# A scan kernel: halving the slots of a product on GpSimd before VectorE sums them

## The chip, the cores and the metric

One core of a Trainium2 chip runs the whole program. The time is device microseconds (us) of one execution. The engines named below are TensorE (PE, with its weight loads PEld), VectorE (DVE), ScalarE (ACT), GpSimd (POOL) and the queue of DMA transfers on SyncE (SP).

## What is computed

The reference is a chain of an image network, an attention, a mixture of experts, a memory layer trained at test time and a second mixture of experts. The change lies in the memory layer, a scan over 96 tokens for a batch of 32. Cut to its core:

```python
def loss_fn(params, kk, vv):
    pred = _mlp(params, kk)
    return jnp.mean((pred - vv) ** 2)

def step(carry, xs):
    cp, cm = carry
    k_t, v_t, q_t, a_t, th_t, e_t = xs
    g = jax.vmap(jax.grad(loss_fn))(cp, k_t, v_t)
    s = lambda c: c[:, :, None]
    nm = jax.tree_util.tree_map(lambda m, gg: m * s(e_t) - s(th_t) * gg, cm, g)
    np_ = jax.tree_util.tree_map(lambda p, m: p * (1.0 - s(a_t)) + m, cp, nm)
    out_t = jax.vmap(_mlp, in_axes=(0, 0))(np_, q_t)
    ...
```

`_mlp` is two matrix products with a silu between them. The kernel never forms the weights of the later steps: each gradient is an outer product, so it keeps the vectors (the hidden gradients dz, the hidden values h and the output gradients dy) and adds up their weighted contributions.

## The kernel before, in words

The scan is `memory_scan`, L1378 to L1926. The 96 steps are cut into 6 chunks of 16 (chunk 0 to 5); within a chunk the place of a step is its slot, 0 to 15. Contributions of earlier chunks come from TensorE. Contributions of the chunk's own earlier slots come from elementwise work over a history tile with 16 slots per value: in slot i, n = max(i, 1) slots count. The batch is worked in two halves, g = 0 and g = 1, which leapfrog: while one half waits for TensorE or ScalarE, VectorE works on the other.

VectorE takes its instructions in the order in which they are written. One step (`one_step` of the vector block) issues: silu of half 1 (L1748 to L1751); `output` and `output_end` of half 0 (L1733 to L1739, L1760 to L1805); `hidden_before` of half 0 for the next step (L1718, L1719); `output` of half 1; `gradient_scores` of half 0 (the second L1733 to L1739); `hidden_before` of half 1; `output_end` of half 1; then the gradients, and the hidden values and the silu of half 0 of the next step.

`hidden_before` is the reader that matters here. It waits for a semaphore of GpSimd and sums a product over its slots:

```python
dve.wait_ge(zprod_ready, 2 * (t - c - 1) + g + 1)
n = max(t - c * NC - 1, 1)
s.link(V.reduce_sum(zsum[:, g, :], z_prod[:, g, :, :].rearrange("p a (b s) -> p (a b) s", s=NC)[:, :, 0:n], AX.X))
s.mark(V.tensor_tensor(quads(z_before[:, g, :]), quads(zsum[:, g, :]), base_at(g, t), ALU.add))
```

GpSimd writes that product. Its step (`one_step` of the gpsimd block, L1506 to L1536) issues, also in order: from chunk 1 on two small weights `wm` (L1511); the two `y_w` (L1519, each after VectorE's L1803 has read the previous one); for each half two products `prod` with the new hidden value (L1525), their sum (L1528), and the slope of the silu (L1529 to L1532); and last the two products `z_prod` (L1536), 32 values by n slots, for the next step. L1525 to L1528 already use a semaphore `halves_ready` for the order of a product and a sum on GpSimd itself.

TensorE's order in a step is forward scores of half 0, forward past 0, forward scores 1, backward scores 0 (which waits for L1805 of half 0), forward past 1, backward past 0, backward scores 1, backward past 1. VectorE waits for forward past at L1792 and for backward scores at the second L1733.

Of the kernel before, what the change touches and what calls it, by code (L numbers as in the profile page):

```python
# [7 lines left out]
ALU = mybir.AluOpType  # L8
# [11 lines left out]
def bc(ap, *shape):  # L20

    return ap.broadcast_to(list(shape))
# [1061 lines left out]
NC = 16  # L1084
# [293 lines left out]
def memory_scan(nc, M, H_room, hist_y, ident, cols_in, rows_in, own_in):  # L1378
# [12 lines left out]
    GW = QB * NC  # L1391
    APART = 4
    with ExitStack() as ctx:
# [10 lines left out]
        hist_h, hist_dz = sb("hist_h", [128, 2, 2, NB, NC]), sb("hist_dz", [128, 2, 2, NB, NC])  # L1404
# [5 lines left out]
        prod, z_prod = (room[:, n * 1024:(n + 1) * 1024].rearrange("p (g a x) -> p g a x", g=2, a=2) for n in range(2))  # L1410
# [4 lines left out]
        g_row = sb("g_row", [128, 2, NB * NC])  # L1415
# [22 lines left out]
        upto = lambda x, g, c, n: x[:, c % 2, :, :, 0:n].rearrange("p a (c b) s -> p a c b s", c=2)[:, :, :, QB * g:QB * (g + 1), :]  # L1438
        part = lambda x, n: x.rearrange("p (b s) -> p b s", s=NC)[:, :, 0:n]
        four = lambda x, n: x.rearrange("p a (c b s) -> p a c b s", c=2, s=NC)[:, :, :, :, 0:n]  # L1440
        over = lambda x, n: bc(x.rearrange("p (c b s) -> p c b s", c=2, s=NC)[:, :, :, 0:n].unsqueeze(1), 128, 2, 2, QB, n)
# [6 lines left out]
        summed, zprod_ready, dz_ready, pool_step, wm_ready = sem("summed"), sem("zprod_ready"), sem("dz_ready"), sem("pool_step"), sem("wm_ready")  # L1448
        halves_ready = sem("halves_ready")
# [11 lines left out]
        with nc.Block() as block:  # L1461
            @block.sync
            def _(sp):
                sp.dma_start(cols[:, :, :], cols_in).then_inc(ones_in, 16)
                sp.dma_start(rows_[:, :, :], rows_in).then_inc(ones_in, 16)
                sp.dma_start(own[:, :], own_in).then_inc(ones_in, 16)
                for c in range(NCH):
                    def rows(k, t, turn):
                        if turn is not None:
                            sp.wait_ge(yw_ready, 2 * turn)  # L1470
                            sp.wait_ge(z_ready, 2 * turn)
                        for b2 in range(2):
                            sp.dma_start(w_row[b2 * DM:(b2 + 1) * DM, k, :],
                                         M["w_rows"][bass.ds(t, 1), c, b2 * HB:(b2 + 1) * HB, :].rearrange("t b s -> t (b s)").broadcast_to([DM, HB * NC])).then_inc(w_in[k], 16)
                        sp.dma_start(g_row[:, k, :], M["g_rows"][bass.ds(t, 1), c, :, :].rearrange("t b s -> t (b s)").broadcast_to([128, NB * NC])).then_inc(g_rows_in[k], 16)

                    if c == 0:
                        for k in range(2):
                            rows(k, k, None)
                        with sp.Fori(1, NC // 2) as i:  # L1480
                            for k in range(2):
                                rows(k, 2 * i + k, 2 * i + k - 1)
                    else:
                        with sp.Fori(0, NC // 2) as i:
                            for k in range(2):
                                rows(k, c * NC + 2 * i + k, c * NC + 2 * i + k - 1)
                for n in range(2):
                    sp.wait_ge(dumped[n], 16 * NCH)

            @block.gpsimd  # L1490
            def _(pool):
                P = nc.gpsimd
                for t in (hist_h, hist_dz):
                    P.memset(t[:, :, :, :, :], 0.0).then_inc(zeroed, 1)
                P.memset(hist_y[:, :, :, :], 0.0).then_inc(zeroed, 1)
                P.memset(dy_now[:, :, :, :], 0.0).then_inc(zeroed, 1)
                P.memset(y_prod[:, :, :], 0.0).then_inc(zeroed, 1)
                P.memset(room[:, 0:1024], 0.0).then_inc(zeroed, 1)
                pool.wait_ge(zeroed, 6)
                pool.wait_ge(ones_in, 48)  # L1500
                for c in range(NCH):
                    pool.wait_ge(g_rows_in[0], (c * NC // 2) * 16 + 16)
                    if c >= 2:
                        pool.wait_ge(zeroed, 6 + c - 1)

                    def one_step(i, k, last):  # L1506
                        t, n = c * NC + i, max(i, 1)
                        if c >= 1:
                            pool.wait_ge(dz_ready, 2 * t - 2)
                            for g in range(2):  # L1510
                                ins = P.tensor_tensor(wm[:, k, g, 0:c, :].rearrange("p c (q b) -> p c q b", q=2),  # L1511
                                                      bc(M["w_bs"][:, 0:c, :, t:t + 1].rearrange("p c (q h) t -> p c q (h t)", q=2)[:, :, :, g:g + 1], 128, c, 2, QB),
                                                      bc(own[:, :].unsqueeze(1).unsqueeze(1), 128, c, 2, QB), ALU.mult)
                                ins.then_inc(wm_ready, 1)
                        pool.wait_ge(w_in[k], (t // 2) * 32 + 32)
                        for g in range(2):

                            pool.wait_ge(yprod_ready, 2 * t + g + 1)
                            P.tensor_tensor(part(y_w[:, g, :], n), part(w_row[:, k, g * GW:(g + 1) * GW], n), hist_y[:, c, g * QB:(g + 1) * QB, 0:n], ALU.mult).then_inc(yw_ready, 1)  # L1519
                        for g in range(2):  # L1520
                            pool.wait_ge(h_ready, 2 * t + g + 1)
                            pool.wait_ge(h_stored, 2 * t if i else 2 * t + g + 1)
                            now = h_now[:, g, 0, :].rearrange("p (a c b) -> p a c b", a=2, c=2).unsqueeze(4)
                            for a in range(2):
                                ins = P.tensor_tensor(four(prod[:, g, :, :], n)[:, a], upto(hist_h, g, c, n)[:, a], bc(now[:, a], 128, 2, QB, n), ALU.mult)  # L1525
                            ins.then_inc(halves_ready, 1)
                            pool.wait_ge(halves_ready, 2 * t + g + 1)
                            P.tensor_tensor(four(prod[:, g, :, :], n)[:, 0], four(prod[:, g, :, :], n)[:, 0], four(prod[:, g, :, :], n)[:, 1], ALU.add).then_inc(prod_ready, 1)  # L1528
                            P.tensor_tensor(hg[:, g, :], h_now[:, g, 0, :], sg[:, g, :], ALU.mult)  # L1529
                            P.tensor_tensor(hs[:, g, :], h_now[:, g, 0, :], sg[:, g, :], ALU.add).then_inc(pool_step, 1)  # L1530
                            pool.wait_ge(pool_step, 2 * t + g + 1)
                            P.tensor_tensor(slope[:, g, :], hs[:, g, :], hg[:, g, :], ALU.subtract).then_inc(slope_ready, 1)  # L1532
                        if not last:
                            pool.wait_ge(g_rows_in[1 - k], ((t + 1) // 2) * 16 + 16)
                            for g in range(2):
                                P.tensor_tensor(four(z_prod[:, g, :, :], n), upto(hist_dz, g, c, n), over(g_row[:, 1 - k, 2 * GW * g:2 * GW * (g + 1)], n), ALU.mult).then_inc(zprod_ready, 1)  # L1536

                    for i in range(NC):
                        one_step(i, i % 2, i == NC - 1)
                    if 1 <= c < NCH - 1:  # L1540
                        pool.wait_ge(dumped[(c - 1) % 2], 32 * ((c - 1) // 2 + 1))
                        pool.wait_ge(turned, 5 * c)
                        P.memset(hist_dz[:, (c + 1) % 2, :, :, :], 0.0).then_inc(zeroed, 1)
# [151 lines left out]
            def _(dve):  # L1695
# [3 lines left out]
                s = Steps(dve, step)  # L1699
# [11 lines left out]
                for c in range(NCH):  # L1711
                    base_at = lambda g, t: M["z_base"][:, :, :, bass.ds(t, 1)].rearrange("p a (c b) s -> p a c (b s)", c=2)[:, :, :, QB * g:QB * (g + 1)]

                    def hidden_before(s, g, t):

                        dve.wait_ge(zprod_ready, 2 * (t - c - 1) + g + 1)
                        n = max(t - c * NC - 1, 1)
                        s.link(V.reduce_sum(zsum[:, g, :], z_prod[:, g, :, :].rearrange("p a (b s) -> p (a b) s", s=NC)[:, :, 0:n], AX.X))  # L1718
                        s.mark(V.tensor_tensor(quads(z_before[:, g, :]), quads(zsum[:, g, :]), base_at(g, t), ALU.add))  # L1719

# [129 lines left out]
                    if c >= 1:  # L1850
# [22 lines left out]
                        for j, (src, parts, left) in work:  # L1873
                            dve.wait_ge(mid_ready, 4 * (c - 1) + j + 1)
                            dve.wait_ge(rest_ready, 4 * (c - 1) + j + 1)
                            ins = V.tensor_tensor(parts(2), left, parts(1), ALU.subtract)
# [11 lines left out]
                    s = Steps(dve, step, start)  # L1888
# [313 lines left out]
```

## Time and profile before

| what | us |
|---|---|
| median of 3 runs (4443.79 to 4450.76) | 4450.04 |
| the profiled execution | 4450.9 |
| its span, first to last instruction | 4448.7 |
| scan, first to last step on the trace, about | 2403 to 3969 |
| busy in the whole span: PE, PEld, DVE, ACT, POOL | 3744.6, 3132.7, 2504.3, 549.9, 740.6 |

The shares over the whole span mix stages: the image network takes the first 40% and the scan about 35%. The scan is looked at by itself, chunk by chunk, and inside a chunk by the timeline of two engines side by side.

### The profile page before, as it was taken

The page shows a single profiled execution, that of the slowest core. Times are in us where ns is not written, and L with a number is a line of the kernel's source. Part 1 is how long each engine was busy: PE and PEld are TensorE (multiplying, and loading weights), DVE is VectorE, ACT ScalarE, POOL GpSimd, SP SyncE. Part 2 cuts the span into 40 slices and gives each one's busy share as a digit, 9 for nine tenths or more (in the row PEclk, how much of TensorE's full clock was granted, in tenths as well). Part 3 has the DMA queues.
Part 4 walks back from the last instruction along what each step waited for, and adds up shares of the span by engine and source line. Part 5 has one row for each costly group of instructions (what it writes and reads, how often), then busy time and mean ns, then how long its engine had stood idle before and what let it go on. Part 6 is the DMA issues. An engine that isn't in the chain of part 4 may idle for free. (4 is left out here: it accounts for less than half of the span.)

```text
span 4448.7 us, 109537 instructions
## 1 busy us (share of the span) xinstructions
PE 3744.6 (84%) x44268; PEld 3132.7 (70%) x44268; DVE 2504.3 (56%) x8138; ACT 549.9 (12%) x1173; POOL 740.6 (17%) x1900
## 2 busy tenths in 40 slices
PE   6999999999999999697656566687998878859587
PEld 5898988769989887454424455687997778857444
DVE  4454545145455452223756888888787887852413
ACT  0101011310010112211211110101001000001011
POOL 1000000000000000000002434334343332332021
PEclk9999999999999999777855555555555555556589
DMA  1010000000000000100003110111000000021111
GB/s 37 16 17 2 16 2 16 2 6 16 2 16 16 2 1 2 25 0 4 0 10 91 32 35 29 31 29 31 26 25 32 22 29 24 22 75 46 21 39 27
DMA packets 189736, 96.97 MB, mean 22 GB/s; under 512 B 139463, under 2 KB 172535, under 8 KB 188632
## 3 DMA queue, kind: packets, MB, share of 16 engines
q1 hardware_dynamic: 183574, 84.19, 8.1%
q10 hardware_dynamic: 4626, 7.39, 0.4%
q8 instruction: 147, 2.41, 0.2%
q0 software_dynamic: 1280, 2.10, 0.2%
q14 instruction: 109, 0.89, 0.1%
HBM read 76.11 MB, written 15.96 MB: 21 GB/s over the span
## 5 line engine op out<-in xcount | busy, mean ns | idle before, releaser
L349 PEld LDWEIGHTS im_acc<-im_cwt,im_chan 128*128 128x128 f32 x2048 | 268.7, 191 | 123.0 <-issue 117.3
L468 ACT ACTIVATE im_a<-im_acc 128x512 f32<-128x512 f32 x256 | 152.9, 597 | 1376.7 <-PE im_acc L349 1376.7
L204 POOL DMA_DIRECT2D image_rows<-im_ho x16 | 9.6, 603 | 1761.2 <-DVEq L459 1761.2
L445 DVE COPY im_chan<-im_ring 128x512 f32<-128x512 f32 x192 | 132.8, 692 | 286.8 <-PE im_ring L296 286.8
L346 PE MATMUL im_acc<-im_u,im_e 97*128 97x512 f32 x512 | 265.3, 599 | 7.6 <-DVE im_u L439 7.6
L349 PE MATMUL im_acc<-im_cwt,im_chan 128*128 x2048 | 270.1, 274 | 0.0
L258 PE MATMUL im_ring<-im_d,im_a 128*128 128x128 f32 (+1 forms) x2048 | 242.5, 281 | 19.1 <-issue 12.9
L258 PEld LDWEIGHTS im_ring<-im_d,im_a 128*128 128x128 f32 x2048 | 239.5, 198 | 22.1 <-issue 18.5
L1641 PE MATMUL sc_ps<-H,sc_cols 128*128 128x128 f32 x768 | 231.2, 457 | 11.9 <-POOL H L1528 11.5
L439 DVE COPY im_u<-im_ring 80x512 f32<-80x512 f32 x256 | 171.6, 685 | 118.8 <-PE im_ring L290 118.8
L406 DVE COPY im_half_t<-im_ring 128x480 f32<-128x480 f32 x192 | 168.5, 903 | 116.5 <-PE im_ring L258 116.5
L1662 PE MATMUL sc_ps<-sc_y_prod,sc_rows 128*128 128x128 f32 x768 | 230.6, 456 | 0.0
L290 PE MATMUL im_ring<-im_e,im_half_t 80*80 80x128 f32 x2048 | 229.0, 273 | 0.0
L290 PEld LDWEIGHTS im_ring<-im_e,im_half_t 80*80 80x80 f32 x2048 | 224.6, 150 | 0.4
L1525 POOL TENSOR_TENSOR H<-sc_hist_h,sc_h_now 128x16 f32<-128x16 f32 (+14 forms) x384 | 147.7, 404 | 462.8 <-DVE sc_h_now L1748 365.9
L1648 PE MATMUL sc_ps<-sc_coef_y,sc_dy_t 128*128 128x16 bf16 x2880 | 105.4, 176 | 116.8 <-DVE sc_coef_y L1739 116.3
L1648 PEld LDWEIGHTS sc_ps<-sc_coef_y,sc_dy_t 128*128 128x128 bf16 x2880 | 99.5, 106 | 147.1 <-DVE sc_coef_y L1739 142.6
L1575 ACT ACTIVATE sc_sg<-sc_z 128x32 f32<-128x32 f32 x192 | 43.9, 229 | 1271.1 <-DVE sc_z L1726 1236.8
L296 PE MATMUL im_ring<-ident,im_a 128*128 128x128 f32 x1280 | 192.8, 280 | 1.4 <-ACT im_a L468 1.4
L1641 PEld LDWEIGHTS sc_ps<-H,sc_cols 128*128 128x128 f32 x768 | 178.2, 322 | 14.9 <-POOL H L1528 14.4
L277 PE MATMUL im_ring<-im_spec,im_wbd 128*128 128x128 f32 x1600 | 180.7, 275 | 0.0
L277 PEld LDWEIGHTS im_ring<-im_spec,im_wbd 128*128 128x128 f32 x1600 | 179.3, 192 | 1.1 <-issue 0.2
(394 smaller groups left out, 7460.3 us busy)
## 6 DMA issues: line engine op xcount, KB each, us to landing
sc_g_row<-mem_g_rows_dram SPq DMA_DIRECT2D x96, 256.0 KB, 3.5
im_wbd<-in_c_mix_dram SPq DMA_DIRECT2D x32, 400.0 KB, 6.1
sc_w_row<-mem_w_rows_dram SPq DMA_DIRECT2D x192, 64.0 KB, 2.5
sw_g_all<-sw_gates SPq DMA_DIRECT2D x8, 768.0 KB
mem_hist_h_dram<-sc_hist_h ACTq DMA_DIRECT2D x6, 512.0 KB, 3.0
mem_hist_dz_dram<-sc_hist_dz ACTq DMA_DIRECT2D x6, 512.0 KB, 3.7
mo_hist_dz<-mem_hist_dz_dram SPq DMA_DIRECT2D x8, 384.0 KB, 6.4
mo_hist_h<-mem_hist_h_dram SPq DMA_DIRECT2D x8, 384.0 KB, 6.5
```

The lines of the kernel that those rows point to most:

```text
L258: mm = MM(ps[:, i * 80:i * 80 + n], a[:, g, c, :], d1[:, 0:n], start=True, stop=True)
L277: mm = MM(ps[:, i * 32:i * 32 + 128], wbd[:, m, :], spec[:, m:m + 4, :].rearrange("p m b -> p (m b)"), start=True, stop=True)
L290: mm = MM(ps[0:80, i * 128:(i + 1) * 128], half_t[0:80, g % 2, (q + i) * 80:(q + i + 1) * 80], e1[:, :], start=True, stop=True)
L296: mm = T(ps[:, m * 128:(m + 1) * 128], a[:, g, :, :].rearrange("p c (w x) -> p (c w) x", x=32)[:, :, p * 4 + m], ident[:, :])
L346: MM(acc[:, p % 2, :], e2[0:97, :], u[:, p, :, :].rearrange("p o w -> p (o w)"), start=True, stop=True, skip_group_check=True)
L349: mm = MM(acc[:, p % 2, m:512:4], chan[:, p % 2, m * 128:(m + 1) * 128], cwt[:, bass.ds(l, 1), :].rearrange("p a c -> p (a c)"), start=Fal ...
L406: V.tensor_copy(half_t[:, g % 2, :].rearrange("p (n c) -> p c n", c=C)[:, q:q + w, :], src).then_inc(drained, 1)
L439: V.tensor_copy(u[0:80, :, q:q + 4, :], src).then_inc(drained, 1)
L468: nc.scalar.activation(a[:, g, :, :].rearrange("p c (w x) -> p (c w) x", x=32)[:, :, p * 4:p * 4 + 4], acc[:, p % 2, :].rearrange("p (c m) ...
L1641: mm = MM(hh(g), cols[:, b2, :], prod[:, g, 0, b2 * GW:(b2 + 1) * GW], start=b2 == 0, stop=b2 == 1)
L1648: mm = MM(past_y(g), dy_t[:, cc, w, g, :], top(coef_y[:, g, m, cc, :]), start=n == 0, stop=n == 6 * c - 1)
L1662: mm = MM(yy(g)[:, b2 * GW:(b2 + 1) * GW], rows_[:, b2, :], y_prod[:, g, :], start=True, stop=True)
```

## The change

After the two products `z_prod` of a slot with n of 4 or more, GpSimd adds the upper n // 2 slots onto the lower n // 2, for each half in two instructions (a = 0, 1). VectorE's reduction then reads only n - n // 2 slots. The products count on `halves_ready`, which orders GpSimd's adds behind them, and the second add of a half counts on `zprod_ready`, for which VectorE waits. `halves(t)` is the number of counts before step t. For n below 4 nothing changes.

```diff
+                    halves = lambda t: 2 * t + 2 * (NC - 5) * (t // NC) + 2 * max(t % NC - 4, 0)
+
                     def one_step(i, k, last):
...
-                            pool.wait_ge(halves_ready, 2 * t + g + 1)
+                            pool.wait_ge(halves_ready, halves(t) + g + 1)
...
                             for g in range(2):
-                                P.tensor_tensor(four(z_prod[:, g, :, :], n), upto(hist_dz, g, c, n), over(g_row[:, 1 - k, 2 * GW * g:2 * GW * (g + 1)], n), ALU.mult).then_inc(zprod_ready, 1)
+                                P.tensor_tensor(four(z_prod[:, g, :, :], n), upto(hist_dz, g, c, n), over(g_row[:, 1 - k, 2 * GW * g:2 * GW * (g + 1)], n), ALU.mult).then_inc(halves_ready if n >= 4 else zprod_ready, 1)
+                            for g in range(2 if n >= 4 else 0):
+                                slots = lambda a, lo, hi: z_prod[:, g, a, :].rearrange("p (b s) -> p b s", s=NC)[:, :, lo:hi]
+                                pool.wait_ge(halves_ready, halves(t) + 2 + g + 1)
+                                for a in range(2):
+                                    ins = P.tensor_tensor(slots(a, 0, n // 2), slots(a, 0, n // 2), slots(a, n - n // 2, n), ALU.add)
+                                ins.then_inc(zprod_ready, 1)
...
                         n = max(t - c * NC - 1, 1)
+                        n = n - n // 2 if n >= 4 else n
                         s.link(V.reduce_sum(zsum[:, g, :], z_prod[:, g, :, :].rearrange("p a (b s) -> p (a b) s", s=NC)[:, :, 0:n], AX.X))
```

GpSimd's order at slot 14 of chunk 2, before (`H` is the room that `prod` and `z_prod` share):

```order
L1529 TENSOR_TENSOR sc_hg<-sc_h_now,sc_sg 128x32
L1530 TENSOR_TENSOR sc_hs<-sc_h_now,sc_sg 128x32
L1532 TENSOR_TENSOR sc_slope<-sc_hs,sc_hg 128x32
L1536 TENSOR_TENSOR H<-sc_hist_dz,sc_g_row 128x32x14 x2
L1511 TENSOR_TENSOR sc_wm<-mem_w_bs,sc_own 128x32 x2
L1519 TENSOR_TENSOR sc_y_w<-sc_w_row,hist_y 128x8x15 x2
```

The same place with the change:

```order
L1531 TENSOR_TENSOR sc_hg<-sc_h_now,sc_sg 128x32
L1532 TENSOR_TENSOR sc_hs<-sc_h_now,sc_sg 128x32
L1534 TENSOR_TENSOR sc_slope<-sc_hs,sc_hg 128x32
L1538 TENSOR_TENSOR H<-sc_hist_dz,sc_g_row 128x32x14 x2
L1543 TENSOR_TENSOR H<-H 128x16x7 x4
L1513 TENSOR_TENSOR sc_wm<-mem_w_bs,sc_own 128x32 x2
L1521 TENSOR_TENSOR sc_y_w<-sc_w_row,hist_y 128x8x15 x2
```

Four adds of 16 by 7 elements stand between the products and the next step's `wm` and `y_w`.

In chunk 0, which has no `wm`, the same slot with the change reads:

```order
L1531 TENSOR_TENSOR sc_hg<-sc_h_now,sc_sg 128x32
L1532 TENSOR_TENSOR sc_hs<-sc_h_now,sc_sg 128x32
L1534 TENSOR_TENSOR sc_slope<-sc_hs,sc_hg 128x32
L1538 TENSOR_TENSOR H<-sc_hist_dz,sc_g_row 128x32x14 x2
L1543 TENSOR_TENSOR H<-H 128x16x7 x4
L1521 TENSOR_TENSOR sc_y_w<-sc_w_row,hist_y 128x8x15 x2
```

Here the adds stand right ahead of `y_w`. On the other engines the order is as before; on VectorE L1718 reads fewer slots.

## Rows read from the trace of the kernel before

**Rows 1.** Busy time by stretch, here chunks 0, 2 and 3 (columns in the first line).

```profile
core 0: us, PE busy (x) PEld busy (x) DVE busy (x) ACT busy (x) POOL busy (x), PEclk, DMA share, GB/s
2403.00:2582.00 179.00, 95.56 (x944) 76.07 (x944) 151.06 (x697) 26.14 (x73) 84.56 (x239) 0.50 0.13 34
2859.00:3106.00 247.00, 204.79 (x4882) 188.82 (x4883) 206.68 (x1026) 19.24 (x73) 98.21 (x287) 0.52 0.09 26
3134.00:3390.00 256.00, 242.29 (x6472) 231.10 (x6468) 202.55 (x971) 22.21 (x76) 95.24 (x269) 0.51 0.09 28
```

**Rows 2.** Timeline of VectorE, chunk 2, slot 14 (start, duration, engine, line).

```profile
3077.53 1.94 DVE L1798 SCALAR_TENSOR_TENSOR sc_dy_now<-sc_ysum,sc_rest 64x8 f32<-64x8 f32 x2
3079.49 0.19 DVE L1799 SCALAR_TENSOR_TENSOR hist_y<-sc_ysum,sc_rest 128x8 f32<-128x8 f32 x1
3079.72 0.17 DVE L1801 TENSOR_TENSOR sc_dy_now<-sc_dy_now 128x16 f32<-128x16 f32 x1
3079.81 0.27 DVE L1803 TENSOR_TENSOR sc_y_prod<-sc_y_w,hist_y 128x112 f32<-128x112 f32 x1
3080.00 0.16 DVE L1805 TENSOR_TENSOR sc_dy_now<-sc_dy_now 128x16 f32<-128x16 f32 x1
3080.08 0.61 DVE L1718 TENSOR_REDUCE sc_zsum<-H 128x32 f32<-128x448 f32 x1
3080.72 0.21 DVE L1719 TENSOR_TENSOR sc_z_before<-sc_zsum,mem_z_base 128x32 f32<-128x32 f32 x1
...
3084.29 0.34 DVE L1798 SCALAR_TENSOR_TENSOR sc_dy_now<-sc_ysum,sc_rest 64x8 f32<-64x8 f32 x2
```

**Rows 3.** Timeline of GpSimd, the same stretch.

```profile
3077.17 2.29 POOL L1536 TENSOR_TENSOR H<-sc_hist_dz,sc_g_row 128x448 f32<-128x448 f32 x2
3079.41 0.45 POOL L1511 TENSOR_TENSOR sc_wm<-mem_w_bs,sc_own 128x32 f32<-128x32 f32 x2
3080.22 0.45 POOL L1519 TENSOR_TENSOR sc_y_w<-sc_w_row,hist_y 128x120 f32<-128x120 f32 x1 [0.36 <-DVE sc_y_prod L1803]
```

**Rows 4.** Timeline of VectorE, chunk 0, slot 14.

```profile
2577.28 1.24 DVE L1803 TENSOR_TENSOR sc_y_prod<-sc_y_w,hist_y 128x112 f32<-128x112 f32 x1
2578.44 1.13 DVE L1805 TENSOR_TENSOR sc_dy_now<-sc_dy_now 128x16 f32<-128x16 f32 x1
2579.49 0.61 DVE L1718 TENSOR_REDUCE sc_zsum<-H 128x32 f32<-128x448 f32 x1
2580.13 0.21 DVE L1719 TENSOR_TENSOR sc_z_before<-sc_zsum,mem_z_base 128x32 f32<-128x32 f32 x1
```

**Rows 5.** Timeline of GpSimd, the same stretch of chunk 0.

```profile
2577.23 2.31 POOL L1536 TENSOR_TENSOR H<-sc_hist_dz,sc_g_row 128x448 f32<-128x448 f32 x2
```

**Rows 6.** Groups by form in the scan: L1718 (busy, mean ns, idle before).

```profile
L1718 DVE TENSOR_REDUCE sc_zsum<-H 128x32 f32<-128x448 f32 x12 | 7.3, 610 | 0.0
...
L1718 DVE TENSOR_REDUCE sc_zsum<-H 128x32 f32<-128x224 f32 x12 | 4.5, 379 | 0.0
```

**Rows 7.** Groups by form in the scan: GpSimd's products and in-place adds.

```profile
L1536 POOL TENSOR_TENSOR H<-sc_hist_dz,sc_g_row 128x448 f32<-128x448 f32 x12 | 13.8, 1168 | 0.0
...
L1528 POOL TENSOR_TENSOR H<-H 128x112 f32<-128x112 f32 x12 | 5.3, 439 | 0.9
...
L1528 POOL TENSOR_TENSOR H<-H 128x32 f32<-128x32 f32 x12 | 3.2, 267 | 0.9
```

**Rows 8.** Timeline of VectorE, chunk 3, slot 5, then slot 14: waits of half 1.

```profile
3208.07 0.34 DVE L1792 SCALAR_TENSOR_TENSOR sc_rest<-sc_ps,sc_off 64x8 f32<-64x8 f32 x2 [0.28 <-PE sc_ps L1648]
...
3210.86 0.21 DVE L1733 TENSOR_TENSOR sc_coef_h<-sc_ps,sc_wm 128x48 f32<-128x48 f32 x1 [0.76 <-PE sc_ps L1658]
...
3357.00 0.33 DVE L1792 SCALAR_TENSOR_TENSOR sc_rest<-sc_ps,sc_off 64x8 f32<-64x8 f32 x2
```

**Rows 9.** Waits in the scan: who waited for whom, us in total, times, longest.

```profile
PEld sc_ps L1655 <- DVE sc_dy_now L1805: 41.5, 66, 1.6
```

**Rows 10.** Groups by form in the scan: two of VectorE's small instructions.

```profile
L1798 DVE SCALAR_TENSOR_TENSOR sc_dy_now<-sc_ysum,sc_rest 64x8 f32<-64x8 f32 x384 | 96.4, 251 | 9.2
...
L1792 DVE SCALAR_TENSOR_TENSOR sc_rest<-sc_ps,sc_off 64x8 f32<-64x8 f32 x320 | 52.1, 163 | 42.6 <-PE sc_ps L1648 37.8 <-issue 0.7 <-DVE sc_ysum L1784 0.4
```

## The prediction
> **What bounds the kernel now.** I read the busy time by stretch first. In chunk 0 VectorE is busy 151 of 179 us and GpSimd 85; in chunk 2 VectorE 207 of 247 with TensorE's 205 beside it; in chunk 3 TensorE leads with 242 of 256 against VectorE's 203 [rows 1]. So VectorE's instruction order sets the pace in the early chunks, TensorE takes part from chunk 3 on, and GpSimd looks as if it had room. The question is what GpSimd's room is worth, and for that I put two timelines side by side.
>
> In chunk 2, slot 14, the pair L1798 lasts 1.94 us [rows 2]. The same pair for the other half, with GpSimd idle, lasts 0.34 [rows 2]. Nothing in its operands differs. GpSimd's two products L1536 run from 3077.17 to 3079.46 [rows 3], and the pair ends at 3079.47. By the products' mean of 1.17 us, the first ended near 3078.34 and the second at 3079.46 [rows 3, 7]: the first instruction of the pair waited out the first product, the second waited out the second. L1798 reads two tiles of SBUF. L1792, of the same shape but with one operand in PSUM, has a mean of 163 ns, against 251 for L1798 [rows 10]. The reduction L1718 reads one tile of SBUF and is not stretched: 0.61 beside `y_w`, its mean being 610 ns [rows 2, 3, 6].
>
> In chunk 0, slot 14, it is L1803 and L1805 that meet the products: 1.24 and 1.13 us, with L1805 ending at 2579.57 where the products end at 2579.54 [rows 4, 5]. So **a VectorE instruction with two SBUF inputs, met by a running GpSimd instruction, ends just after it; and back-to-back GpSimd instructions let through one VectorE instruction each.** `wm`, two ops of about 0.2 us, does the same to L1799 and L1801, which costs little since it is so short [rows 2, 3].
>
> The page "SBUF — State Buffer" of the Trainium skill, section "Who interferes with whom", says that a VectorE instruction with two SBUF inputs contends with a GpSimd instruction that reads SBUF, that the later of the two blocks fully, and that a reduction does not contend. The rows above agree, and this rule speaks against the change: by it moved work is not free, by busy shares alone it would be.
>
> **The change part by part.** *Shorter reductions.* From 448 to 224 elements L1718 goes from 610 to 379 ns [rows 6], 231 ns for 7 slots, or 33 ns a slot. The slots removed are n // 2 for n = 4 to 14: 2, 2, 3, 3, 4, 4, 5, 5, 6, 6, 7, together 47. That is 1.55 us for one half in one chunk and 18.6 us for two halves and 6 chunks. This is the most that the change can give.
>
> *Four adds on GpSimd*, in 11 slots of each chunk, 264 in all. They have the shape of L1528: 267 ns for 16 x 2 elements, 439 for 16 x 7 [rows 7], between them on a line. Followed by another, an instruction costs about 0.04 less: two products take 2.29, not 2 x 1.168 = 2.34 [rows 3, 7]. So four adds take 0.91 (n = 4) to 1.60 us (n = 14); their sum over the 11 slots is 13.4 us a chunk. The new waits on `halves_ready` cost nothing by themselves: the product of half 0 is done a whole product earlier, that of half 1 two adds earlier.
>
> The page "Perfetto Trace Analysis" of the Trainium skill, section "GPSIMD Engine Instruction", calls the span of a GpSimd instruction unreliable and asks for start-to-start spacing. By spans the sum would rise by 4 x 0.04 x about 45 exposed slots, 7 us; by spacing it stands as worked out here.
>
> *Chunks 1 and 2, where L1799 to L1805 come after the products.* Before, L1805 ended at 3080.16, 0.70 after the products [rows 2, 3]. With the adds, L1799, L1801, L1803 and L1805 meet one add each, and L1805 ends 0.03 after the fourth. The delay is 4 adds - 0.67: 0.24 us at n = 4, 0.93 at n = 14, in a chunk 13.4 - 7.4 = 6.0 us. Of that the two reductions give back 3.1. The net is 2.9 a chunk, **5.8 us** for both. Is L1805 on the path? TensorE's weight loads for the backward scores waited for it 66 times of the 160 in chunks 1 to 5 [rows 9], and VectorE itself is in order, so everything behind L1805 moves with it.
>
> *Chunk 0.* There the four instructions have met the products already, so L1805 hardly moves. But the reduction of half 0 started at 2579.49, with the products' end, and now waits for two adds, and L1719 behind it reads two SBUF tiles and meets adds three and four. At slot 14 it ended at 2580.34 and will end at 2579.54 + 1.60 + 0.03 = 2581.17: 0.83 later, of which the second reduction gives back 0.23. In slots 9 to 14 the same sum (4 adds + 0.03 - reduction - 0.19) gives 8.3 + 0.2 - 3.2 - 1.1 = 4.2, less 1.1 for the second reductions: 3.1. In slots 4 to 8 the products are shorter and VectorE comes to the reduction some time after them, so part of the adds is over by then; I choose 0 to 0.2 a step, 0.7 (bounds: nothing, and slot 9's 0.4 in each, 2.0). Together **3.8 us**.
>
> *Chunks 3 to 5.* In the low slots VectorE waits for TensorE behind both reductions: 0.28 us at L1792 and 0.76 at L1733 in chunk 3, slot 5; at slot 14 L1792 waits no longer [rows 8]. There neither a delay of 0.3 nor a gain of 0.13 reaches the end: zero, covered by TensorE's scores of half 1. From slot 10 on I take the sum of chunk 1: 7.2 - 3.4 - 1.9 = 1.9 a chunk, **5.7 us**.
>
> *What stands behind the adds.* `wm` and `y_w` move back by the length of the adds. SyncE's row loads wait for the `y_w` of half 1, before which GpSimd still idles for microseconds, so they are safe. But `y_w` of half 0, 0.45 us, ran beside the reduction, which it cannot stop [rows 2, 3]; now its place is beside L1719, which it can. Bounds: nothing, and 0.45 in each of 45 exposed steps, 20 us. `wm` ends first in most steps and lets L1719 through, so I take **2 us**, near the low end.
>
> The sum is 5.8 + 3.8 + 5.7 + 2 = **+17.3 us**. On the profiled 4450.9 that is 4468.2; the median of the runs shown lies 0.9 below, so I say 4468. A measurement of this kernel can tell about 0.2% from no change, 9 us.
>
> **The rivals.** *GpSimd's adds do not hold VectorE.* They are short, and between adds VectorE's instructions may slip in by twos. Then chunks 1 to 5 keep their savings, 5 x 3.1, less what TensorE hides in slots 4 to 9 of chunks 3 to 5 (18 slots x 0.033 x 2 x 3 = 3.6), so -11.9; chunk 0 still waits for two adds, +2.5: 4441.5. Against it: one instruction per product in three places of the rows above, and the same even at `wm`'s 0.2 us.
>
> *TensorE absorbs it.* If the slack of chunk 3's low slots held elsewhere, only chunk 0 would pay: 4450.9 + 3.8, 4455. For it: waits for TensorE occur in most steps. Against it: L1792 of half 1 has none at slot 14 even in chunk 3 [rows 8], and the large delays are in the late slots.
>
> *More is held than the four.* If L1719 meets `y_w` every time, or the pair L1798 itself starts late enough for L1805 to be pushed onto `wm`, each exposed step loses up to 0.45 more: +20, 4488. This decides wherever VectorE reaches L1798 during the second product instead of the first.
>
> **How the numbers follow.** The forecast as worked out has 0.70. Adds that hold nothing (4441.5): 0.04. TensorE absorbs it (4455): 0.11. More is held (4488): 0.15. The range from 4455 to 4484 leaves out the first rival and the end of the last, and takes in both sides of the 2 us. Faster by over 0.2% is the first rival's end only, 0.04; within 0.2% is mostly the second, 0.12; slower by over 0.2% has 0.84.
>
> **What would show it.** Right: in chunk 2, slot 14, L1799 to L1805 each last about 0.4 us and end with one add each; L1718 there takes 0.38; in chunk 0, slot 14, L1718 of half 0 shows idle time ahead of it that GpSimd ends, some 0.8 us; the low slots of chunk 3 are as long as before; the added line has 264 instructions between 0.27 and 0.44 us. Wrong: L1799 to L1805 stay at 0.2 beside the adds (then the first rival), or the waits at L1792 shrink by what L1805 is late (then the second).

## The result, and the profile after

The changed kernel takes **4471.1 us** (median of 12 runs, 4457.2 to 4478.7) against 4450.1 for the kernel before (12 runs beside it): a ratio of 1.0041, with a 95% interval of 1.0029 to 1.0053. That is slower: by 21 us between the medians, by 13 to 24 within the interval, where the forecast was 17.

In chunks 0, 2 and 3 GpSimd's busy time rises by 12 to 13 us each, against [rows 1], and VectorE's by 3 in chunks 2 and 3, although its reductions are shorter (the columns are named in the first line):

```profile
core 0: us, PE busy (x) PEld busy (x) DVE busy (x) ACT busy (x) POOL busy (x), PEclk, DMA share, GB/s
2411.00:2594.00 183.00, 95.51 (x944) 76.02 (x944) 149.94 (x698) 26.31 (x73) 97.22 (x283) 0.50 0.11 33
2874.00:3124.00 250.00, 205.58 (x4881) 188.58 (x4880) 209.66 (x1025) 19.23 (x73) 110.52 (x331) 0.52 0.09 26
3154.00:3412.00 258.00, 240.47 (x6422) 228.56 (x6418) 205.86 (x969) 21.73 (x74) 106.87 (x311) 0.51 0.09 27
```

The lines have moved: L1798, L1799, L1801, L1803 and L1805 are now L1807, L1808, L1810, L1812 and L1814; the reduction L1718 and the add L1719 are L1727 and L1728; VectorE's two waits for TensorE, L1792 and L1733, are now at L1801 and L1742; the products are L1538, the four adds L1543, `wm` L1513, `y_w` L1521. This is VectorE in chunk 2, slot 14, the place of [rows 2]:

```profile
3095.78 1.94 DVE L1807 SCALAR_TENSOR_TENSOR sc_dy_now<-sc_ysum,sc_rest 64x8 f32<-64x8 f32 x2
3097.73 0.39 DVE L1808 SCALAR_TENSOR_TENSOR hist_y<-sc_ysum,sc_rest 128x8 f32<-128x8 f32 x1
3098.16 0.37 DVE L1810 TENSOR_TENSOR sc_dy_now<-sc_dy_now 128x16 f32<-128x16 f32 x1
3098.45 0.58 DVE L1812 TENSOR_TENSOR sc_y_prod<-sc_y_w,hist_y 128x112 f32<-128x112 f32 x1
3098.95 0.41 DVE L1814 TENSOR_TENSOR sc_dy_now<-sc_dy_now 128x16 f32<-128x16 f32 x1
3099.28 0.37 DVE L1727 TENSOR_REDUCE sc_zsum<-H 128x32 f32<-128x224 f32 x1
3099.68 0.52 DVE L1728 TENSOR_TENSOR sc_z_before<-sc_zsum,mem_z_base 128x32 f32<-128x32 f32 x1
```

And GpSimd in the same stretch, the place of [rows 3]:

```profile
3095.41 2.29 POOL L1538 TENSOR_TENSOR H<-sc_hist_dz,sc_g_row 128x448 f32<-128x448 f32 x2
3097.65 1.67 POOL L1543 TENSOR_TENSOR H<-H 128x112 f32<-128x112 f32 x4
3099.28 0.44 POOL L1513 TENSOR_TENSOR sc_wm<-mem_w_bs,sc_own 128x32 f32<-128x32 f32 x2
3099.69 0.44 POOL L1521 TENSOR_TENSOR sc_y_w<-sc_w_row,hist_y 128x120 f32<-128x120 f32 x1
```

Four instructions that took 0.16 to 0.27 us take 0.37 to 0.58, one for each add, and L1814 ends at 3099.36 beside the fourth add's 3099.32. It ends 1.66 us after the products; before it was 0.70. The reduction gives back 0.24. L1728 then meets `y_w` and takes 0.52 where L1719 took 0.21.

In chunk 0, slot 14 (the place of [rows 4]) the reduction of half 0 now stands idle for 0.81 us, and GpSimd's adds end that wait, as the bracket in its row says:

```profile
2588.82 1.24 DVE L1812 TENSOR_TENSOR sc_y_prod<-sc_y_w,hist_y 128x112 f32<-128x112 f32 x1
2589.98 1.13 DVE L1814 TENSOR_TENSOR sc_dy_now<-sc_dy_now 128x16 f32<-128x16 f32 x1
2591.91 0.39 DVE L1727 TENSOR_REDUCE sc_zsum<-H 128x32 f32<-128x224 f32 x1 [0.81 <-POOL H L1543]
2592.34 0.42 DVE L1728 TENSOR_TENSOR sc_z_before<-sc_zsum,mem_z_base 128x32 f32<-128x32 f32 x1
```

GpSimd beside it, the place of [rows 5]:

```profile
2588.77 2.31 POOL L1538 TENSOR_TENSOR H<-sc_hist_dz,sc_g_row 128x448 f32<-128x448 f32 x2
2591.04 1.64 POOL L1543 TENSOR_TENSOR H<-H 128x112 f32<-128x112 f32 x4
```

In chunk 3, slot 5, VectorE's two waits for TensorE are still there, 0.35 and 0.77 us for 0.28 and 0.76 in [rows 8]: the low slots of chunk 3 are neither longer nor shorter.

```profile
3226.94 0.34 DVE L1801 SCALAR_TENSOR_TENSOR sc_rest<-sc_ps,sc_off 64x8 f32<-64x8 f32 x2 [0.35 <-PE sc_ps L1656]
...
3229.73 0.21 DVE L1742 TENSOR_TENSOR sc_coef_h<-sc_ps,sc_wm 128x48 f32<-128x48 f32 x1 [0.77 <-PE sc_ps L1666]
```

TensorE's weight loads wait longer for the late L1814, 52.4 us for 41.5 [rows 9] (us in total, times, longest):

```profile
PEld sc_ps L1663 <- DVE sc_dy_now L1814: 52.4, 75, 2.6
```

**Where the time is.** A step's length is taken from one start of the silu of half 1 (L1748 in the kernel before) to the next. This table gives, for every kernel of the study, the step lengths less those of the kernel before, summed over slots 4 to 14 of each chunk, in one profiled execution each, in us:

```
                     chunk 0     1      2      3      4      5    total
after                 +4.06  +4.05  +2.99  +1.75  +2.90  +2.14   +17.88
e1_adds_beside        +1.92  +6.80  +6.22  +4.26  +4.90  +3.57   +27.67
e2_short_only         -3.12  -3.07  -3.07  -1.21  -2.55  -1.83   -14.85
e3_one_add            +2.37  +3.34  +3.20  +2.71  +2.84  +2.29   +16.75
e4_memsets            -0.05  +0.23  -0.03  +0.18  -0.82  -0.57    -1.06
e5_late_product       -2.86  -2.88  -2.46  -1.13  -1.85  -1.12   -12.31
e6_late_product_z     -5.86  -6.58  -5.64  -1.84  -4.80  -3.59   -28.32
e7_late_wm            -0.14  +0.04  -0.25  -0.21  -0.94  -0.64    -2.12
e8_late_product_adds  -3.28  -6.62  -5.42  -1.49  -1.75  -1.87   -20.43
```

The steps account for the result: +17.9 of a measured +13 to +24. The span of the profiled execution is longer by 25 (4473.9); 8 of that lie before the scan, which begins at 2411 instead of 2403 though nothing changed there, and belong to the execution.

### The profile page after: what moved, and what is told of

It reads as the page before. It is cut to its first block and busy times, and to the rows that moved or that the text cites. A ratio compares the mean times of both kernels' runs of the same rounds, so it can differ in the third digit from the quotient of the medians.

```text
span 4473.9 us, 109801 instructions
## 1 busy us (share of the span) xinstructions
PE 3757.7 (84%) x44268; PEld 3135.2 (70%) x44268; DVE 2517.2 (56%) x8138; ACT 550.0 (12%) x1173; POOL 814.4 (18%) x2164
## 5 line engine op out<-in xcount | busy, mean ns | idle before, releaser
L1649 PE MATMUL sc_ps<-H,sc_cols 128*128 128x128 f32 x768 | 230.9, 456 | 11.8 <-POOL H L1530 11.4
```

What stands on the lines that cost most here:

```text
L1649: mm = MM(hh(g), cols[:, b2, :], prod[:, g, 0, b2 * GW:(b2 + 1) * GW], start=b2 == 0, stop=b2 == 1)
```

## The experiments

**The adds without the gain.** The kernel before, with the same 264 adds written to a spare tile; the reductions stay as long as they were and don't wait for the adds.

```diff
+        spare = sb("spare", [128, 2, 2, 112])
...
+                            for g in range(2 if n >= 4 else 0):
...
+                                pool.wait_ge(zprod_ready, 2 * (t - c) + g + 1)
+                                for a in range(2):
+                                    P.tensor_tensor(spare[:, g, a, 0:16 * (n // 2)].rearrange("p (b s) -> p b s", b=16), slots(a, 0, n // 2), slots(a, n - n // 2, n), ALU.add)
```

> The kernel before, plus the change's 264 adds on GpSimd, written to a spare tile that nobody reads; VectorE's reductions read all slots as before and wait for the products alone. Theory A (the adds hold VectorE's instructions with two SBUF inputs, one each): no reduction waits for an add, and still the scan grows by about 26 us (22 to 30): what the change lost plus the savings it no longer has. Chunk 1 about +6.8, chunk 2 about +5.7, chunk 0 only +2 to +3, chunks 3 to 5 +3 to +5 each; in chunk 2, slot 14, L1799 to L1805 last 0.35 to 0.6 us each; ratio to before 1.005 to 1.007. Theory B (the loss is the reductions' longer wait for GpSimd's adds): nothing waits for them here, so the time is that of before, ratio 0.999 to 1.001.

Measured: 4474.7 us, 1.0055 [1.004, 1.007]. The adds cost time although nothing uses what they write. VectorE in chunk 2, slot 14 (lines L1805 to L1811 answer to L1799 to L1805):

```profile
3091.51 0.39 DVE L1805 SCALAR_TENSOR_TENSOR hist_y<-sc_ysum,sc_rest 128x8 f32<-128x8 f32 x1
3091.93 0.37 DVE L1807 TENSOR_TENSOR sc_dy_now<-sc_dy_now 128x16 f32<-128x16 f32 x1
3092.23 0.58 DVE L1809 TENSOR_TENSOR sc_y_prod<-sc_y_w,hist_y 128x112 f32<-128x112 f32 x1
3092.72 0.41 DVE L1811 TENSOR_TENSOR sc_dy_now<-sc_dy_now 128x16 f32<-128x16 f32 x1
```

GpSimd beside it:

```profile
3091.43 1.67 POOL L1542 TENSOR_TENSOR sc_spare<-H 128x112 f32<-128x112 f32 x4
```

The four durations are those of the changed kernel, to the hundredth. So it is the adds beside them, and no semaphore or dependence, that stretch them.

**The gain without the adds.** The kernel before, with reductions over the lower n - n // 2 slots alone; the upper slots are left out of the sum.

```diff
                         n = max(t - c * NC - 1, 1)
+                        n = n - n // 2 if n >= 4 else n
```

> The kernel before, with VectorE's reduction reading n - n // 2 slots and no adds on GpSimd (the upper slots are left out of the sum). Theory A: the whole saving of 18.6 us less what TensorE hides in the low slots of chunks 3 to 5 (3.6): about -15 us, ratio 0.9966, some 3.1 us in each of chunks 0 to 2. Theory C (TensorE's answers end last in most steps, so VectorE's work is mostly covered): -5 us or less, ratio above 0.999.

Measured: 4434.8 us, 0.9956 [0.9941, 0.9971]; 14.9 us by steps. Of the 18.6 that the prediction gives as the most, 3.7 do not show, nearly all of it in chunks 3 to 5; there VectorE idles 3.4 us longer for TensorE than before (slots 4 to 14), so TensorE hides them. Together the two runs rebuild the change. In chunks 1 to 5 e1 gives +25.8 and e2 -11.7, sum +14.0; the change gives +13.8 there. In chunk 0 the sum is -1.2 and the change gives +4.1. The 5.3 between them goes with what neither run has, the reduction waiting for the adds' own result. In the changed kernel's scan that wait has 5.1 us in 10 times, all of them in chunk 0:

```profile
DVE sc_zsum L1727 <- POOL H L1543: 5.1, 10, 0.8
```

**One add for two.** The changed kernel, with one add of 32 values x n // 2 slots for each half, in place of two of 16.

```diff
-                                slots = lambda a, lo, hi: z_prod[:, g, a, :].rearrange("p (b s) -> p b s", s=NC)[:, :, lo:hi]
+                                slots = lambda lo, hi: z_prod[:, g, :, :].rearrange("p a (b s) -> p (a b) s", s=NC)[:, :, lo:hi]
...
-                                for a in range(2):
-                                    ins = P.tensor_tensor(slots(a, 0, n // 2), slots(a, 0, n // 2), slots(a, n - n // 2, n), ALU.add)
-                                ins.then_inc(zprod_ready, 1)
+                                P.tensor_tensor(slots(0, n // 2), slots(0, n // 2), slots(n - n // 2, n), ALU.add).then_inc(zprod_ready, 1)
```

> The changed kernel with one add of 32 x n // 2 a half in place of two of 16 x n // 2: by the rows of the in-place sum two adds then take 0.56 us (n = 4) to 1.27 (n = 14) where four took 0.91 to 1.6. Theory A: a held instruction is let through once per GpSimd instruction, so in chunks 1 to 5 L1799 and L1801 meet the two adds and L1803 and L1805 meet wm instead; L1805 ends where it did, to 0.1 us. Only chunk 0, which has no wm, gains some 2 us, and slots 13 and 14 gain 0.3 where L1719 no longer meets y_w: the scan is 4 to 5 us shorter than with the change, ratio to before 1.003. Theory D (VectorE loses as much time as GpSimd spends on adds, however cut): 0.3 us less in each of some 45 slots, 13 us shorter than with the change, ratio to before 1.000 to 1.001.

Measured: 4469.6 us, 1.0039 [1.0024, 1.0054], 1.1 us better by steps than the change. The large gain is not there, and of the small one only chunk 0's part (-1.7) and a piece in chunk 1 (-0.7). VectorE in chunk 2, slot 14 (L1806 to L1812 answer to L1799 to L1805):

```profile
3095.62 0.65 DVE L1806 SCALAR_TENSOR_TENSOR hist_y<-sc_ysum,sc_rest 128x8 f32<-128x8 f32 x1
3096.30 0.62 DVE L1808 TENSOR_TENSOR sc_dy_now<-sc_dy_now 128x16 f32<-128x16 f32 x1
3096.85 0.26 DVE L1810 TENSOR_TENSOR sc_y_prod<-sc_y_w,hist_y 128x112 f32<-128x112 f32 x1
3097.03 0.21 DVE L1812 TENSOR_TENSOR sc_dy_now<-sc_dy_now 128x16 f32<-128x16 f32 x1
```

GpSimd beside it:

```profile
3093.30 2.28 POOL L1538 TENSOR_TENSOR H<-sc_hist_dz,sc_g_row 128x448 f32<-128x448 f32 x2
3095.54 1.35 POOL L1542 TENSOR_TENSOR H<-H 128x224 f32<-128x224 f32 x2
3096.85 0.57 POOL L1513 TENSOR_TENSOR sc_wm<-mem_w_bs,sc_own 128x32 f32<-128x32 f32 x2
```

Two adds hold two instructions, 0.65 and 0.62 us, and the next two run beside `wm`'s two. L1812 ends at 3097.24, 1.66 us after the products, exactly as with four adds in 1.67 us: what the shorter adds gave, `wm` took. In chunk 3 this kernel is 1.0 us slower than the change; why was not found.

**GpSimd busy, but reading nothing.** The kernel before, with four memsets in place of the adds, as long as these.

```diff
+        spare = bf("spare", [128, 2, 2, 416])
+        LENGTH = {2: 200, 3: 225, 4: 265, 5: 320, 6: 365, 7: 410}
...
+                            for g in range(2 if n >= 4 else 0):
+                                for a in range(2):
+                                    P.memset(spare[:, g, a, 0:LENGTH[n // 2]], 0.0)
```

> The kernel before, plus four memsets of a spare tile of 0.25 to 0.45 us each where the change has its adds: GpSimd is as busy and wm and y_w come as late, but nothing of SBUF is read. Theory A, in the form that the contention is for the read of SBUF: L1799 to L1805 last 0.16 to 0.27 us beside the memsets, as before; what is left is y_w and wm in a new place, +2 to +10 us, ratio 1.0005 to 1.002. Theory E (GpSimd's occupation itself, or the lateness of wm and y_w, is the loss): as in the run with adds beside, some +20 to +26 us, ratio 1.005.

Measured: 4449.8 us, 0.999 [0.9978, 1.0002]. VectorE in chunk 2, slot 14 (L1804 to L1808 answer to L1799 to L1803):

```profile
3082.19 1.94 DVE L1803 SCALAR_TENSOR_TENSOR sc_dy_now<-sc_ysum,sc_rest 64x8 f32<-64x8 f32 x2
3084.15 0.17 DVE L1804 SCALAR_TENSOR_TENSOR hist_y<-sc_ysum,sc_rest 128x8 f32<-128x8 f32 x1
3084.36 0.18 DVE L1806 TENSOR_TENSOR sc_dy_now<-sc_dy_now 128x16 f32<-128x16 f32 x1
3084.45 0.27 DVE L1808 TENSOR_TENSOR sc_y_prod<-sc_y_w,hist_y 128x112 f32<-128x112 f32 x1
```

GpSimd beside it:

```profile
3084.05 1.58 POOL L1541 MEMSET sc_spare<- 128x410 bf16 x4
```

With 1.58 us of memsets beside them the instructions keep 0.17, 0.18 and 0.27 us, while the pair L1803 ahead of them is stretched by the products as ever. So what holds VectorE is GpSimd's reading of SBUF, not its being busy. (A memset does no arithmetic either; no run here tells the two apart.) The page "SBUF — State Buffer" of the Trainium skill, section "Who interferes with whom", says just this, that the contention is with a GpSimd instruction that reads SBUF and not with one that only writes it; this trace agrees. A small loss of 2 to 10 us had been expected. By the time there is no difference; by steps a small gain of 1.1 us came, and it lies in chunks 4 and 5. A later run takes that up.

**Moving a reader away.** If the hold is the cause, the product of half 1, which was there before the change, should cost as the adds do, and moving it should win. In the kernel before, it is issued after `wm` and after VectorE's L1803 of half 0, just ahead of `y_w` of half 0; it then runs beside the reduction.

```diff
+                    def product(i, k, g):
+                        n = max(i, 1)
+                        P.tensor_tensor(four(z_prod[:, g, :, :], n), upto(hist_dz, g, c, n), over(g_row[:, 1 - k, 2 * GW * g:2 * GW * (g + 1)], n), ALU.mult).then_inc(zprod_ready, 1)
...
                             pool.wait_ge(yprod_ready, 2 * t + g + 1)
+                            if g == 0 and i >= 1:
+                                product(i - 1, 1 - k, 1)
...
-                            for g in range(2):
-                                P.tensor_tensor(four(z_prod[:, g, :, :], n), upto(hist_dz, g, c, n), over(g_row[:, 1 - k, 2 * GW * g:2 * GW * (g + 1)], n), ALU.mult).then_inc(zprod_ready, 1)
+                            product(i, k, 0)
```

> The kernel before, without the change; GpSimd issues z_prod of half 1 after wm and after VectorE's L1803 of half 0, ahead of y_w, in place of right behind z_prod of half 0. Theory A: L1798 meets one product and wm, no longer two products; in chunk 2, slot 14, L1805 ends some 0.75 us sooner, but L1719 then meets the late product and gives half of it back: 0.2 to 0.4 us a late slot, -6 to -12 us in all, ratio 0.9975 to 0.9985. Theory F (GpSimd's work holds VectorE equally wherever it stands in the step): no change, ratio 0.9995 to 1.0005.

Measured: 4441.2 us, 0.9967 [0.9956, 0.9979]: faster, a little more than expected. For the moved product one instruction now pays, the add behind the reduction (L1724, 0.21 us before) in chunk 2, slot 14:

```profile
3072.55 0.73 DVE L1724 TENSOR_TENSOR sc_z_before<-sc_zsum,mem_z_base 128x32 f32<-128x32 f32 x1
```

The moved product beside it:

```profile
3072.05 1.17 POOL L1508 TENSOR_TENSOR H<-sc_hist_dz,sc_g_row 128x448 f32<-128x448 f32 x1 [0.57 <-DVE sc_y_prod L1808]
```

**That add moved too.** The kernel of the last run, in which the add of half 0 is now done with that of half 1, so that what follows the reduction of half 0 reads PSUM.

```diff
...
-                        s.mark(V.tensor_tensor(quads(z_before[:, g, :]), quads(zsum[:, g, :]), base_at(g, t), ALU.add))
+                        for h in range(2 * g):
+                            s.mark(V.tensor_tensor(quads(z_before[:, h, :]), quads(zsum[:, h, :]), base_at(h, t), ALU.add))
```

> As the run with the late product, and VectorE forms z_before of half 0 (L1719) together with that of half 1, so that behind the reduction of half 0 come L1733 and L1760, which read one SBUF tile each. Theory A: the late product now runs beside the reduction, L1733 and L1760 and holds only the end of L1736; 0.5 to 0.8 us a late slot in chunks 0 to 2, about -5 in each of these chunks and -1 to -2.5 in each of chunks 3 to 5 where TensorE comes last: -18 to -22 us in all, ratio 0.995 to 0.996. Theory F: no change, ratio 0.9995 to 1.0005.

Measured: **4418.8 us, 0.9919 [0.9904, 0.9935]**, which beats both kernels. VectorE in chunk 2, slot 14 (L1804 is the pair L1798, L1723 the reduction; L1739 and L1766 have an operand in PSUM, `sc_ps`):

```profile
3060.69 1.02 DVE L1804 SCALAR_TENSOR_TENSOR sc_dy_now<-sc_ysum,sc_rest 64x8 f32<-64x8 f32 x2
...
3062.31 0.61 DVE L1723 TENSOR_REDUCE sc_zsum<-H 128x32 f32<-128x448 f32 x1
3062.96 0.19 DVE L1739 TENSOR_TENSOR sc_coef_y<-sc_ps,sc_wm 128x32 f32<-128x32 f32 x1
3063.07 0.33 DVE L1766 SCALAR_TENSOR_TENSOR sc_pred<-sc_ps,mem_c_f 64x8 f32<-64x8 f32 x2
```

GpSimd beside it:

```profile
3060.32 1.16 POOL L1508 TENSOR_TENSOR H<-sc_hist_dz,sc_g_row 128x448 f32<-128x448 f32 x1
3061.44 0.45 POOL L1515 TENSOR_TENSOR sc_wm<-mem_w_bs,sc_own 128x32 f32<-128x32 f32 x2
3062.45 1.16 POOL L1508 TENSOR_TENSOR H<-sc_hist_dz,sc_g_row 128x448 f32<-128x448 f32 x1 [0.57 <-DVE sc_y_prod L1809]
```

The second product, 1.16 us, lies beside a reduction and two instructions that read PSUM, and none of the three is stretched; the pair takes 1.02 us for 1.94. The steps gave 28.3 us where 18 to 22 had been expected: chunks 0 to 2 gave 18.1 for about 15, and chunks 4 and 5 gave 4.8 and 3.6 where 1 to 2.5 each had been allowed, so too much of the scan had been put down to TensorE. The ratio stands for 29 to 43 us, more than the steps hold. In the profiled executions another 8.8 us lie after the start of the scan's last step (488.0 us to the end, 496.8 before). That stretch is 488 to 504 us long in the executions of this study, though none of the kernels changes anything behind the scan, so the gain in the scan is nearer 28 us than 36.

**Where the memsets' small gain came from.** They also moved `wm`. This run moves `wm` alone, behind `y_w` of half 0.

```diff
-                        if c >= 1:
+                        def weights():
...
+                            if g == 0 and c >= 1:
+                                weights()
```

> The kernel before, with GpSimd's wm behind the y_w of half 0 in place of ahead of it, as the memsets had moved it in effect. Theory A: L1799 and L1801 are no longer held by wm (0.02 to 0.05 us each in chunks 1 and 2, where they ran nearly in step with it; 0.1 to 0.3 in the late slots of chunks 4 and 5, where a pair of instructions met it), and wm may hold L1719 or L1736 instead: 0 to -3 us, as with the memsets, mostly in chunks 4 and 5; ratio 0.9993 to 1.000. If the gain of the memset run in chunks 4 and 5 had another cause, these chunks do not change here.

Measured: 4452.5 us, 0.9993 [0.9981, 1.0005], no difference by the time; by steps -0.94 and -0.64 in chunks 4 and 5, close to the memsets' -0.82 and -0.57, and little elsewhere. So `wm`'s place would explain their gain, as far as single executions can show so small a thing.

**The adds in a better place.** The kernel of 4418.8 us, with the change's adds right behind each product, and the shorter reductions.

```diff
...
+                        if n >= 4:
+                            pool.wait_ge(halved, 22 * c + 2 * (n - 4) + g + 1)
...
+                            for a in range(2):
+                                ins = P.tensor_tensor(slots(a, 0, n // 2), slots(a, 0, n // 2), slots(a, n - n // 2, n), ALU.add)
+                            ins.then_inc(zprod_ready, 1)
...
+                        n = n - n // 2 if n >= 4 else n
```

> The faster version (late product, z_before of half 0 formed later) with the change's adds put back, the two of each half right behind its product. Theory A: the two adds of half 0 hold two more of L1798 to L1805 (0.45 us at n = 4, 0.8 at n = 14, and about 0.1 for the wait on the product just issued), those of half 1 hold L1736, L1764 or L1739 of the next half; the shorter reductions give back 0.13 to 0.46. Some 0.6 to 1.2 us a slot from n = 4 in chunks 0 to 2, half of that in chunks 3 to 5: +25 to +45 us over the run without adds, ratio to before 0.998 to 1.002. If the order of the products alone had made the adds costly (they hold nothing once the products no longer come back to back), the savings stay: 10 to 15 us below the run without adds, ratio 0.989.

Measured: 4428.4 us, 0.9939 [0.9926, 0.9952], between the two expectations. Against the same kernel without adds it loses 7.9 us by steps, though the two intervals overlap: 2.6 in chunk 0, 3.1 and 1.7 in chunks 4 and 5, 0.3 in chunk 3, and in chunks 1 and 2 it comes out even. In chunk 0 the old wait is back; at slot 13:

```profile
2568.54 0.39 DVE L1730 TENSOR_REDUCE sc_zsum<-H 128x32 f32<-128x224 f32 x1 [0.71 <-POOL H L1513]
```

In chunk 4, slot 14, VectorE meets the second product and its adds in instructions with two SBUF inputs:

```profile
3628.59 0.48 DVE L1746 TENSOR_TENSOR sc_coef_y<-sc_score_sum,sc_wm 128x64 f32<-128x64 f32 x1
...
3629.51 0.42 DVE L1777 SCALAR_TENSOR_TENSOR sc_off<-mem_v_y,sc_pred 128x8 f32<-128x8 f32 x1
3629.96 0.42 DVE L1752 TENSOR_TENSOR sc_coef_y<-sc_coef_y 128x64 f32<-128x64 f32 x1
```

GpSimd beside it:

```profile
3629.06 0.84 POOL L1513 TENSOR_TENSOR H<-H 128x112 f32<-128x112 f32 x2
```

Without the adds these three take 0.35, 0.16 and 0.23 us. They lose 0.58, and the four small instructions beside half 0's adds and the `wm` behind them lose 0.37 more; two shorter reductions win 0.48, and the step is 0.50 longer. The adds don't pay even there. Theory A, with 25 to 45 us, was too dark for every chunk.

## Why the prediction was right

Forecast 4468, measured 4471; +17.3 us forecast, +17.9 by steps. Point by point:

- *The mechanism.* L1799 to L1805 (now L1808 to L1814) each end with one add, and L1805's delay in chunk 2, slot 14 is 1.66 - 0.70 = 0.96 us, against 0.93 in the prediction. e1 shows that the adds alone do it, e4 that it is their reading.
- *The largest saving, 18.6.* e2 gave 14.9; the rest is hidden by TensorE. In chunks 1 to 5 the prediction's terms make a price of 25.4 us (6.0 twice, 3.8 three times, and the 2 for `y_w`) and a saving of 11.9 (3.1 twice, 1.9 three times). Taken apart, e1 gave +25.8 there and e2 -11.7, so both sides were of the right size, and not their difference alone.
- *Chunk 0, +3.8.* Measured +4.1, by the wait that was named. L1728 ends 1.68 us after the products at slot 14; 1.63 was worked out.
- *Chunks 1 and 2, +5.8, chunks 3 to 5, +5.7, and 2 for `y_w` anywhere.* Measured +7.0 and +6.8: 13.8 against 13.5. Slot by slot, chunk 3 changes by 0.02 us or less in slots 4 to 9, as was said, and from slot 10 on it loses 0.20 to 0.52 a step.
- *The small term, and some luck.* L1728 meets `y_w` far more often than was said: in chunk 1 in slot 4 and from slot 9 on, in chunk 2 in slots 4 to 7, 13 and 14, in chunk 3 in slots 6, 7, 8 and 10, in chunk 4 from slot 8, in chunk 5 from slot 9 but for slot 10. This is chunk 1, slot 12:

```profile
2805.13 0.46 DVE L1728 TENSOR_TENSOR sc_z_before<-sc_zsum,mem_z_base 128x32 f32<-128x32 f32 x1
```

GpSimd beside it:

```profile
2805.12 0.41 POOL L1521 TENSOR_TENSOR sc_y_w<-sc_w_row,hist_y 128x104 f32<-128x104 f32 x1
```

L1728's mean rises from 215 to 247 ns, which over 180 instructions is 5.8 us: 0.8 in chunk 0, where it meets the adds instead, and 5.0 in chunks 1 to 5, nearly all with `y_w`, where 2 had been put. The reason given, that `wm` lets L1728 through in most steps, holds in slots 5 to 8 of chunk 1, 8 to 12 of chunk 2 and 12 to 14 of chunk 3. That the sum came out all the same is luck in part: in slots 10 to 14 of chunks 3 to 5 L1814 of half 0 came 9.7 us late in all, counted from the start of its step, where the prediction had taken 11.4.
- *Spacing against spans.* By spans the sum would have been 7 us higher. Four adds of 445 ns by their group mean take 1.67 us, not 1.78. The Trainium skill's "Perfetto Trace Analysis", section "GPSIMD Engine Instruction", warns against going by spans and asks for the spacing; the trace agrees.

```profile
L1543 POOL TENSOR_TENSOR H<-H 128x112 f32<-128x112 f32 x24 | 9.9, 445 | 0.0
...
L1728 DVE TENSOR_TENSOR sc_z_before<-sc_zsum,mem_z_base 128x32 f32<-128x32 f32 x180 | 44.4, 247 | 6.2
```

Of the rivals, "GpSimd's adds do not hold VectorE" falls by e1. "TensorE absorbs it" falls by the steps of chunks 1 to 5; it holds in slots 4 to 9 of chunk 3 and 4 to 8 of chunk 5, as the forecast had it, but chunk 4 loses 0.8 us in slots 6 to 9, where the forecast had nothing. "More is held" is true in part, by the 5.0 us of L1728 and not by 20 (and its 4488 counts the 2 us twice that stand in the forecast already).

## What to carry to other kernels

Idle time on GpSimd is not free for work that reads SBUF: where VectorE runs instructions with two SBUF inputs beside it, each of GpSimd's instructions holds one of them to its own end (in this kernel 0.16 to 0.27 us became 0.37 to 0.58), so the price of moved work is counted from the two engines' timelines side by side and not from busy shares. Before moving work to GpSimd, look at what it already holds. Here, putting an existing product beside a reduction and instructions that read PSUM took 0.81% off the time (0.64% by the steps of the scan), while moving work onto GpSimd added 0.41%.

## What had not been expected

Shortening GpSimd's work from 1.67 to 1.35 us changed the end of VectorE's row by nothing (1.66 us after the products both times), because the next GpSimd instructions, `wm`, moved up into the place. Theory A of that run had said so; not expected was that only 1.1 of its 4 to 5 us came elsewhere. The chunks that had been thrown together as TensorE's differ among themselves: before, TensorE is busy 242 of 256 us in chunk 3 [rows 1], but 203 of 250 in chunk 4 and 225 of 260 in chunk 5 (the same view, 3410 to 3660 and 3680 to 3940 us). Their gains in e6 stand in that order: -1.8 in chunk 3, -3.6 in chunk 5, -4.8 in chunk 4.
